# A gated cross-attention and expert block on one Trainium2 core: inputs turned first in each group of projections, ten weight pieces loaded to where later pieces go, gate products in the attention core, last sequences normed between shared steps

## The reference

```python
# x, context: 16 sequences x 128 tokens x 256; frac: 16 x 128
q, k, v = proj(layernorm(x)), proj(context), proj(context)   # 16 heads of 16
D = clip(frac[k] - frac[q], -0.2, 0.2)
bias = alpha_pos[h] * max(D, 0) + alpha_neg[h] * min(D, 0)
probs = softmax(gamma * (q @ k.T) / 4 + delta * bias)
x = x + tanh(g_xattn) * (probs @ v @ Wo.T + bo)
xf = layernorm(x)                                            # 2048 x 256
top_w, top_i = top_k(xf @ gate_w + gate_b, 2)                # 8 experts
out = sum over the 2 of softmax(top_w) * (gelu(xf @ w1[e] + b1[e]) @ w2[e] + b2[e])
shared = gelu(xf @ ws1 + bs1) @ ws2 + bs2                    # hidden size 1024
x = x + tanh(g_ffn) * (out + shared)
```

## Time and profile before

| | |
|---|---|
| median of 3 runs | 540.45 us (539.53 to 541.78) |
| profiled execution, its own time | 539.68 us |
| its span, first to last instruction | 537.9 us |
| mean granted clock of PE | 0.971 |
| PE busy | 477.4 us, 89% |
| PE weight loads busy | 398.1 us, 74% |
| DVE busy | 371.0 us, 69% |
| ACT busy | 323.9 us, 60% |
| POOL busy | 243.1 us, 45% |
| DMA | 55.45 MB, mean 103 GB/s |

### The profile page before, as it was taken

How to read it: one execution, slowest core, us unless ns; L and a number is a source line. 1 busy time by engine, 2 the same in 40 slices (tenths; PEclk the granted TensorE clock), 3 DMA queues, 4 the chain that set the end, 5 groups by cost and what they waited for, 6 DMA issues and landing times.

```text
span 537.9 us, 17410 instructions
## 1 busy us (share of the span) xinstructions
PE 477.4 (89%) x6358; PEld 398.1 (74%) x6359; DVE 371.0 (69%) x888; ACT 323.9 (60%) x889; POOL 243.1 (45%) x271
## 2 busy tenths in 40 slices
PE   3699689989989989978789799999999999999990
PEld 1356468868778867655455589999999999999980
DVE  5776579878889973597775677666666666666750
ACT  3697288997989988754564754535444444535430
POOL 4747555886855657357671002323223232323231
PEclk9899699998999999999999899999999999999996
DMA  8702225553565322227767443232323222232211
GB/s 259 258 22 78 80 70 149 157 188 116 157 188 176 117 76 80 79 95 207 214 202 158 150 148 50 47 51 39 59 41 57 40 51 46 39 58 39 40 21 20
DMA packets 48548, 55.45 MB, mean 103 GB/s; under 512 B 17138, under 2 KB 39666, under 8 KB 48372
## 3 DMA queue, kind: packets, MB, share of 16 engines
q1 hardware_dynamic: 41348, 45.44, 28.8%
q0 software_dynamic: 7152, 9.34, 9.6%
HBM read 35.95 MB, written 18.82 MB: 102 GB/s over the span
## 4 chain that ended last, share of the span: by engine, by line
PE 50%; ACT 12%; DVE 10%; DMA 10%; POOL 8%; issue 6%; SPq 1%; DVEq 0%; ACTq 0%; POOLq 0%
PE bank L1239 45%; ACT W L682 6%; DMA stage<-wts 3%; PE bank L1338 3%; DMA W<-d_dram 3%; DMA xres<-x 2%; DVE hsplit L1051 2%; POOL W L551 2%; PE bank L1522 2%; POOL xs_dram L606 1%; DVE W L1158 1%; DMA xs_dram<-W,place 1%; ACT W L688 1%; DMA xres<-xs_dram 1%; ACT hbuf L801 1%
## 5 line engine op out<-in xcount | busy, mean ns | idle before, releaser
L836 ACT ACTIVATE hbuf<-bank,b1t 128x128 f32<-128x128 f32 x312 | 88.8, 368 | 113.6 <-PE bank L1239 112.4
L620 POOL DMA_INDIRECT out<-xres,idu x39 | 60.8, 1560 | 184.2 <-DVE xres L1213 170.7
L1239 PE MATMUL bank<-W,xT 128*128 (+1 forms) x1704 | 136.6, 249 | 0.0
L1239 PE MATMUL bank<-xres,W 128*128 128x128 bf16 (+1 forms) x1920 | 125.6, 225 | 5.2 <-DVE xres L884 4.8
L1239 PEld LDWEIGHTS bank<-xres,W 128*128 (+1 forms) x1920 | 112.1, 98 | 14.8 <-issue 8.6
L1239 PEld LDWEIGHTS bank<-W,xT 128*128 128x128 bf16 (+1 forms) x1704 | 113.9, 97 | 12.0
L682 ACT ACTIVATE W<-bank,mx 128x128 f32<-128x128 f32 x256 | 69.4, 394 | 6.7 <-DVE mx L902 6.7
L1239 PE MATMUL bank<-W 128*128 128x17 bf16 (+2 forms) x1376 | 59.1, 188 | 9.6 <-DVE xres L884 4.5
L1239 PE MATMUL bank<-W,hsplit 128*128 128x256 bf16 x432 | 54.6, 276 | 13.4 <-DVE hsplit L1051 11.9
L1239 PEld LDWEIGHTS bank<-W 128*128 128x128 bf16 x1376 | 51.0, 98 | 16.5 <-DVE xres L884 4.8
L1239 PEld LDWEIGHTS bank<-W,hsplit 128*128 128x128 bf16 x432 | 41.7, 99 | 27.9 <-DVE hsplit L1051 18.1
(11 more groups left out here) (144 smaller groups left out, 588.4 us busy)
## 6 DMA issues: line engine op xcount, KB each, us to landing
stage<-wts SPq DMA_DIRECT2D x36, 512.0 KB
xres<-xs_dram SPq DMA_DIRECT2D x39, 128.0 KB, 2.1
xs_dram<-hbuf SPq DMA_DIRECT2D x6, 774.0 KB, 6.4
W<-d_dram SPq DMA_DIRECT2D x32, 128.0 KB, 3.6
W<-ctxT SPq DMA_DIRECT2D x4, 512.0 KB, 8.2
xres<-x SPq DMA_DIRECT2D x4, 512.0 KB, 9.7
d_dram<-W SPq DMA_DIRECT2D x16, 128.0 KB, 2.1
out<-xres SPq DMA_DIRECT2D x4, 512.0 KB, 4.0
```

Source lines behind the costliest of these rows:

```text
L620: nc.gpsimd.indirect_dma_start(out, bass.IndirectOffsetOnAxis(idu[:, par, t:t + 1], axis=0), ysb[par][t], None, compute_op=ALU.add).then_i ...
L836: ins = nc.scalar.activation(hbuf[:, q, c * TR:(c + 1) * TR], bank[UPS * par + q][:, c * TR:(c + 1) * TR], ACT.Gelu, bias=b1t[:, par, UC * ...
L1239: return nc.tensor.matmul(o, a, b, start=start, stop=stop, **kw)
```

## The change

- **Projections.** In each group the inputs come first on all engines, then keys, values, queries. `norm4(g + 1)` stands ahead of the values of group `g`, and `difference_high` behind the queries. `statistics4` on DVE gathers four `stats1` and also adds the epsilon and negates the mean, so that `deviation4` on POOL is two operations. `slopes()` moves from DVE to POOL, between `deviation4(3)` and `clip(2)`. The second load of `x` is issued earlier.
- **Weight pieces.** Ten of them, 18 to 27 (`FAR_PAIRS`), no longer go through `stage`: they are loaded behind the core, all of them without waiting for a conversion, into the parts of `W` where the pieces two pairs later go (`stage_at`), and are converted from there. Pieces 16, 17 and 28 to 35 use `stage`. The last four are converted in the first four tiles, and SP issues the loads of 34 and 35 around those of tiles 4 and 5. Low halves of pieces from 18 on are DVE's.
- **Gate.** For sequences 0 to 11 the gate product stands in the core, in the odd slots, four sequences behind, and the bias is added in `output(b)` one sequence at a time.
- **Last sequences.** `last_tokens` is gone: turning and norming of sequences 13 to 15 is spread over the first shared steps, and their gate follows `shared_down(0)`. Up is three steps ahead (`AHEAD`). The ranks are counted at `m == 2`, the weights' exponential comes at step 5, and ACT runs one small Gelu ahead of `norm2(B - 3)`. `choose` is cut into `logits`, `largest` and `choice`.
- **Tiles.** Four tiles are written out ahead of the loop instead of two.

Moved functions are shown at one engine only, and `slopes()` not at all, since its body stays but for the engine and one operation more:

```diff
-HIGHS_AT = (9, 10, 12, 13, 15, 16, 18, 19, 21, 22, 24, 25, 27, 28, 30, 31)
-LOWS_AT = (10, 11, 13, 14, 16, 17, 19, 20, 22, 23, 25, 26, 28, 29, 31, 32)
-ROWS_AT = (10, 11, 12, 13, 14, 15, 16, 18, 19, 20, 21, 22)
+VECTOR_PIECES = range(NOW + 2, PIECES)
+HIGHS_AT = (6, 9, 11, 13, 15, 17, 19, 20, 21, 22, 23, 25, 27, 29)
+LOWS_AT = (7, 10, 12, 14, 16, 18, 20, 21, 22, 23, 24, 26, 28, 30)
+ROWS_AT = (6, 7, 8, 10, 11, 12, 13, 14, 15, 16, 18, 19, 20, 21)
+FAR_PAIRS = range(9, 14)
...
+AHEAD = 3
+RANKS_AT = 2
+EXP_AT = 5
...
+        def stage_at(m):
+
+            if m // 2 in FAR_PAIRS:
+                at = (m // 2 + 2) * 2 * DC * HID + m % 2 * 2 * HID
+                return W[:, at:at + 2 * HID].bitcast(fp32)
+            return stage[:, m % 2 * HID:(m % 2 + 1) * HID]
...
+                    piece_converted(sp, m - 2 - (2 * len(FAR_PAIRS) if i == FAR_PAIRS[-1] + 1 else 0))
+                sp.dma_start(stage_at(m), wts[m * P:(m + 1) * P, :]).then_inc(ld_st[k], 16)
+
+            def load_far(m):
+                sp.dma_start(stage_at(m), wts[m * P:(m + 1) * P, :]).then_inc(ld_far[m - 2 * FAR_PAIRS[0]], 16)
...
-            load_pieces(NOW, NOW + 6)
+            load_pieces(NOW, NOW + 2)
+            sp.wait_ge(s_ps, R * B)
+            for m in range(18, 20):
+                load_far(m)
+            sp.wait_ge(pv, R * B)
+            for m in range(20, 26):
+                load_far(m)
+            sp.wait_ge(y_ps, B)
+            for m in range(26, 28):
+                load_far(m)
+            load_pieces(28, 30)
             store_group(0)
-            load_pieces(NOW + 6, NOW + 11)
             store_group(1)
-            load_pieces(NOW + 11, PIECES - 4)
+            load_pieces(30, 32)
...
-            load_piece(PIECES // 2 - 2, 0)
...
-            with sp.Fori(2, TILES // 2) as i:
+            load_piece(PIECES // 2 - 1, 0)
+            load_tile(4, 0)
+            load_piece(PIECES // 2 - 1, 1)
+            load_tile(5, 1)
+            with sp.Fori(3, TILES // 2) as i:
...
+                at = slice(4 * g, 4 * g + 4)
+                pool.wait_ge(ln1_moments, g + 1)
+                link(nc.gpsimd.tensor_tensor(rstd1[:, at], rstd1[:, at], mhalf[:, at], ALU.pow))
+                nc.gpsimd.tensor_tensor(nmr[:, at], nmr[:, at], rstd1[:, at], ALU.mult).then_inc(ln1_rstd, 1)
...
-            deviation4(1)
+            context_low(2)
+            deviation4(2)
...
             split_difference(0)
             split_difference(1)
+            deviation4(3)
+            slopes()
             clip(2)
             clip(3)
-            context_low(3)
-            deviation4(3)
...
+            piece_low(NOW // 2, 1)
+            deviation2(B - 1)
 
             for m in range(POOL_SPLITS):
-                if m == 2:
-                    deviation2(B - 1)
                 pool.wait_ge(sh_hi, m + 1)
                 nc.gpsimd.tensor_tensor(hsplit[:, m % DEEP, 1, :], hbuf[:, m % DEEP, :], hsplit[:, m % DEEP, 0, :],
                                         ALU.subtract).then_inc(sh_ready[0], 1)
-                if m in POOL_PIECES_AT:
...
+                piece_loaded(act, 2 * i + k)
+                if i - 2 in FAR_PAIRS:
+                    piece_converted(act, 2 * i - 3)
+                nc.scalar.activation(W[:, piece_at(i, k):piece_at(i, k) + HID], stage_at(2 * i + k), ACT.Copy).then_inc(conv_hi, 1)
...
-            act.wait_ge(ld_cst, 16)
             for g in range(Q4):
+                for c in range(DC):
+                    inputs_high(g, c)
+                if g == 0:
+                    weight_high(0)
+                    act.wait_ge(ld_cst, 16)
                 for o in range(DC):
                     keys_high(g, o)
-                for c in range(DC):
-                    inputs_high(g, c)
+                if g < Q4 - 1:
...
                 if g == 0:
...
-                if g + 1 < Q4:
-                    norm4(g + 1)
+                if g == Q4 - 1:
+                    exponent(0)
+                    exponent(1)
+                for o in range(DC):
+                    queries_high(g, o)
...
-                if g == Q4 - 1:
-                    exponent(0)
-                    exponent(1)
-                for o in range(DC):
...
-                last_tokens(m)
-                if m in PIECES_AT:
-                    q = NOW + 1 + PIECES_AT.index(m)
-                    piece_high(q // 2, q % 2)
-                if m == RANKS_AT:
+                if m == 0:
+                    inputs2_high(B - 2)
+                if m == 1:
+                    norm2(B - 1)
+                if m == 2:
+                    inputs2_high(B - 1)
+                if m == EXP_AT:
...
+                if first(j):
+                    for k in range(4):
+                        act.wait_ge(dispatched[k], 16 * TOPK * B // 4)
+                if first(j, 4):
+                    piece_high((PIECES - 4 + j) // 2, j % 2)
...
+                    stats1(b)
+                at = slice(4 * g, 4 * g + 4)
+                dve.wait_ge(ln1_stat, 4 * g + 4)
+                nc.vector.tensor_scalar(rstd1[:, at], mv1[:, at, 1], EPS, None, ALU.add)
+                nc.vector.tensor_scalar(nmr[:, at], mv1[:, at, 0], -1.0, None, ALU.mult).then_inc(ln1_moments, 1)
...
+                if b >= 4:
+                    logits(b - 4, b - 3)
...
+            statistics4(1)
 
             for g in range(Q4):
+                for c in range(DC):
+                    inputs_low(g, c)
+                if g == 0:
...
-                    slopes()
...
+            payload(0)
+            payload(1)
...
-                    payload(4 + ROWS_AT.index(m))
...
-                if m > HC + 1 and m % HC == 1:
+                    vector_low(VECTOR_PIECES[LOWS_AT.index(m)])
+                if m > HC and m % HC == 2:
...
+                if first(j, 4):
+                    vector_low(PIECES - 4 + j)
...
+                turn_inputs(g)
                 project_keys(g)
-                turn_inputs(g)
...
+                if u % 2 == 1 and b >= 4:
+                    gate(b - 4, b - 3)
                 turn_probs(2 * u)
...
-            shared_up(1)
             turn_o(B - 1)
             turn2(B - 3)
-            gate(0, EARLY_TOKENS)
+            shared_up(1)
+            project_o(B - 1)
+            turn2(B - 2)
...
             for m in range(HC * GROUPS):
-                if m + 2 < HC * GROUPS:
-                    shared_up(m + 2)
+                if m + AHEAD < HC * GROUPS:
+                    shared_up(m + AHEAD)
...
-                last_tokens(m)
+                if m == 0:
+                    pe.wait_ge(x1_ready, B)
+                    gate(EARLY_TOKENS, B)
+                if m == RANKS_AT:
+                    ranks()
```

254 lines of the change are left out of this document (114 added, 140 removed).

## The result

The changed kernel takes 524.64 us, median of four runs (523.94 to 526.24), against 540.31 us of the kernel before: a ratio of 0.9711, 95% interval 0.9678 to 0.9744. The forecast was 533.4 with a range of 526 to 542, so the time lies under the range. The direction was right, the forecast change of 7.0 us a little under half of what came. The profiled execution took 526.24 us with a span of 524.4, against 539.68 and 537.9.

The account below looks back on a forecast made before the run. PE's work bounds the tiles, ACT's exponentials the core; projections and shared steps hold idle time. Terms -0.5 + 3.3 + 0.5 + 0.5 - 13.2 + 2.4 = -7.0 give 532.7 us profiled, 533.4 median, range 526 to 542.

Parts of the forecast that it names:

- Projections: Before the core: ACT blocks behind POOL's slopes and clips, first scores at 58.2; -0.5 us (-4.5 to +2.5).
- Scores of the third sequence: Early core: PE waits for a late difference load at `scores(4)`; +3.3 us (0 to 5).
- Gate in the core: Core: twelve groups of gate matmuls and small DVE additions; +0.5 us (0 to +4.1).
- Last product with the values to `down(6)`: 199.4 to 226.1: gates leave, one up product and new waits come; +0.5 us (-1.5 to +2).
- Shared steps: `down(6)` to first tile: ten direct loads remove most waits, 68.5 us against 81.7; -13.2 us (-16.5 to -5).
- floor of 64.0: Shared steps: PE's own work, 22 pairs 57.2, four downs alone 5.6, first tile's turn and split 1.2 us.
- covered: First tiles: converting pieces 32 to 35 there costs nothing, since ACT and DVE have idle time.
- First tiles: Tile 4's load comes late behind that of piece 34, so PE waits; +2.4 us (0 to +4).
- A: Projections: ACT doesn't wait if POOL finishes clip 3 by 49, `scores(0)` 4 us earlier; 527.4 us, chance 0.17.
- B: Shared steps: payloads held by dispatches at 3.15 us a sequence, costing 7.7 of 13.2 us; 541.1 us, chance 0.16.
- C: Projections: slopes take 5.8 us on POOL, 1.8 more, all on ACT's path; 535.2 us, chance 0.10.
- D: Core: late difference load repeats, 13 more sequences at 1 us; 546.4 us, chance 0.07.

Follow-up runs that it names:

- e1: Changed kernel with up two steps ahead instead of three: 523.92 us, ratio 0.9710.
- e4: Changed kernel with the high half of difference 4 ahead of the first exponentials again, as in the kernel before: 521.22 us, ratio 0.9682.
- e6: Changed kernel with the ten direct loads going through `stage` again and up two steps ahead instead of three: 532.26 us, ratio 0.9897.
- e5: Kernel before with up three steps ahead instead of two, nothing else: 539.53 us, ratio 0.9984.
- e7: Kernel before with DVE's work at steps 9 and 10 (payloads, accumulation, tile table) spread over later steps: 539.36 us, ratio 1.0015.
- e9: Kernel before with pieces 32 to 35 converted in the first four tiles, the other twelve spread over steps 9 to 30: 533.31 us, ratio 0.9862.
- e11: Changed kernel, differences 2 and 3 behind last inputs and keys, 4 behind first exponentials, tiles 4 and 5 before pieces 34 and 35, SP's difference loads first: 510.82 us.
- e8: Changed kernel with the high halves of differences 2 and 3 behind the last inputs and keys on ACT: 516.51 us, ratio 0.9610.

## Why the forecast was wrong

1. **Projections, -0.5 forecast.** The mechanism was right, and its times to half a microsecond. Forecast were the end of `deviation4(3)` at 44.8, the end of ACT's stop near 53.0 and the first scores at 58.2; the trace has 44.3, 53.4 and 58.5. Slopes took 4.5 us on POOL (44.31 to 48.82), between the two bounds of 4.0 and 5.8. The size was off, since one profile stood for the baseline. In six executions with the new projections (changed kernel, e1 to e4, e6) the first scores start between 56.8 and 58.5, in four with the old ones (before, e5, e7, e9) between 58.7 and 60.5. Medians of 57.3 and 59.6 make it -2.3. The profiled pair shows only -0.24, and these 2.1 us would be nearly the whole of the 2.2 by which the medians differ more than the profiled executions.
2. **Scores of the third sequence, +3.3 forecast.** Measured from the first scores it is 22.00 instead of 18.69 us: +3.3. It did not last, as the kernel before loses time to the same kind of wait in later sequences. By the end of the core +2.1 was left. e4 shows the cause of the wait at the third sequence, the place of `difference_high(4)`, and e11 that of the later ones, SP's queue.
3. **Gate in the core, +0.5.** Nothing, by the cadence of 7.85 us in both.
4. **Last product with the values to `down(6)`, +0.5.** Measured: 27.35 against 27.39 us, nothing.
5. **Shared steps, -13.2 forecast, -18.7 measured. This is the step that failed**, in its size and in its cause. The size: 63.0 us were measured where 68.5 were forecast, and the 5.5 us between are two terms of the sum. 4.5 us were left for waits; PE was busy in all but 0.4. 3.5 of them were ACT's `<-remote`, which "nothing removes". It was not in the changed kernel, nor in e5 and e7, which leave this part of the kernel before as it is; it was in e9 (3.8 us) and in e11 (3.0). It may belong to single executions; what brings it stays open. The other 1.0 us is the floor of 64.0: four down products alone were put at 1.41 each, from the starts of weight loads, where PE's pitch is 1.31, and turn and split of the first tile at 1.2 us where they took 0.4. PE's own work is 63.0. The bound of -16.5 rested on the same floor, and so the range ended too high.

   The cause: the forecast gave the gain to the ten direct loads and wrote pieces 32 to 35 off as "covered", with no cost in the tiles, and did not ask what four pieces fewer do where they came from. By the row of kernels above, moving the four pieces gained 10.3 us of the stretch, the direct loads behind it 6.3, the third step 1.4 and the rest of the new order 0.7. In that order the term that the forecast put at nothing is the largest; with the loads first, its share was not measured.
6. **First tiles, +2.4 forecast.** +3.5 in the profiled execution: 1.9 us more of wait for `xres<-xs_dram`, then a first part at 4.33 instead of 2.78 us. In five other executions with the same order the first tiles took 0.3 to 1.9 us longer than before. So +2.4 is inside what came, and above the mean of the six, 1.5.

With the first scores at -0.2 and the rest of the core at +2.1, the six items sum to -13.4 us in the profiled pair. The other 2.2 us of the 15.7 lie between the profiled executions and the medians.

Of the rivals, A ("ACT does not wait") did not happen, but e8 shows that it was worth what it had been given, 6 us: 5.5 by the ratios, 8.1 by the medians. B, dispatches as the new pace, did not happen: PE waited for none of them in the shared steps. C came about a quarter of the way (4.5 between 4.0 and 5.8). Slopes took 4.5 us on POOL against 3.3 on DVE, 1.4 times as long, in 16 operations against 15. The Trainium skill, GPSIMD Engine Reference, section Engine selection, has about two times for elementwise work with two inputs, by which the prediction estimated 6.6 us. This trace has less: the two-input operations of 128x16 take 0.22 us each on POOL and 0.22 and 0.31 on DVE, and the eight of 128x32 1.62 us on POOL against 1.00 on DVE. D, waits at each sequence, came in small: PE's weight loads waited for differences six times, 7.4 us in sum, against four times and 4.7 before.

Of the signs named ahead, the first scores within 57 to 60, ACT's stop, the one wait near 77, no gate group behind the core, no wait for pieces and the wait at tile 4 all came. The one that failed is the one that mattered, 63.0 us from step 6 to the first tile where 66 to 71 were named.
